# Projections, values, router and gate regrouped by rows of weights; features ahead of values

## The reference

```
h = patches(x) @ W.T + b                                  # 768 -> 192
h = h + attn0(layernorm(h))                               # random-feature attention, 12 heads of 16
h = h + experts(layernorm(h))                             # 4 groups x 8 experts, 2 groups chosen, 2 experts in each, hidden 768
h = h + attn1(layernorm(h))                               # rotated queries/keys, causal softmax, 12 heads of 16
h = h + gated_ffn(layernorm(h))                           # shared + 8 gated experts of width 128, 2 chosen

# attn0: q, k, v = split(x @ w_inp + b_inp); s = (q or k) * 16**-0.25 @ omega.T (16 features)
#        f = exp(s - sum(s)/2 - max(s)) + 1e-6; out = causal linear attention(qf, kf, v) @ w_out + b_out
# attn1: q = rope(x @ Wq + bq); k = rope(x @ Wk + bk); v = x @ Wv + bv
#        out = softmax(causal(q k.T / 4)) v @ Wo + bo
```

## Time and profile before

| what | us |
|---|---|
| median of three runs | 474.67 |
| the three runs | 462.99, 477.31, 474.67 |
| span of the profiled execution | 450.5 |
| TensorE busy in that span | 379.3 (84%) |
| vector engine busy | 142.9 (32%) |
| ScalarE busy | 117.0 (26%) |
| GpSimd busy | 71.0 (16%) |

### The profile page before, as it was taken

One profiled execution on the slowest core, in us unless ns is written; L12 is line 12 of the kernel. 1 busy time (PEld: TensorE's weight loads), 2 busy tenths in 40 slices (PEclk: granted clock), 3 DMA queues, 4 the chain that ended last, 5 costly groups with the idle time before them and its releaser, 6 DMA issues. The chain is left out here.

```text
span 450.5 us, 7352 instructions
## 1 busy us (share of the span) xinstructions
PE 379.3 (84%) x2586; PEld 289.1 (64%) x2586; DVE 142.9 (32%) x408; ACT 117.0 (26%) x311; POOL 71.0 (16%) x115
## 2 busy tenths in 40 slices
PE   0879986975587999999999999999910997889995
PEld 0672555954554888888888888888810476753553
DVE  0450025375722111111111111111107558446544
ACT  1301103324023222333322222333210114531110
POOL 0130001000274021122222222222222200000000
PEclk9995556695555899999999999999985796968999
DMA  7649999300023088888889888888213000000001
GB/s 165 155 89 305 243 314 276 74 1 0 25 94 118 8 269 265 259 257 259 274 264 268 263 278 263 256 261 247 90 46 112 1 1 3 1 0 0 1 0 36
DMA packets 66249, 65.81 MB, mean 146 GB/s; under 512 B 10153, under 2 KB 59889, under 8 KB 66225
## 3 DMA queue, kind: packets, MB, share of 16 engines
q1 hardware_dynamic: 63456, 59.39, 46.9%
q0 software_dynamic: 2400, 5.45, 3.3%
q10 hardware_dynamic: 368, 0.66, 0.7%
HBM read 53.45 MB, written 12.03 MB: 145 GB/s over the span
## 5 line engine op out<-in xcount | busy, mean ns | idle before, releaser
L589 ACT ACTIVATE turned<-ps,b1T 128x128 f32<-128x128 f32 x204 | 56.4, 375 | 125.6 <-PE ps L815 125.6
L831 PE MATMUL ps<-w,turned 128*128 128x192 f32 x408 | 71.9, 326 | 0.0
L811 PE MATMUL ps<-fexp,w 128*128 128x128 f32 x408 | 70.1, 295 | 0.0
L831 PEld LDWEIGHTS ps<-w,turned 128*128 128x128 f32 x408 | 65.5, 190 | 0.1
L811 PEld LDWEIGHTS ps<-fexp,w 128*128 128x128 f32 x408 | 55.8, 193 | 8.4 <-issue 0.2
L815 PE MATMUL ps<-fexp,w_tail 64*128 64x128 f32 x408 | 50.5, 324 | 0.0
L1110 DVE COPY fexp<-ps 128x256 f32<-128x256 f32 x34 | 14.4, 425 | 104.3 <-PE ps L801 101.3
L500 POOL DMA_INDIRECT y_picks<-fexp,y_row x34 | 33.1, 974 | 40.5 <-POOL y_row L496 24.7
L815 PEld LDWEIGHTS ps<-fexp,w_tail 64*128 64x128 f32 x408 | 30.9, 186 | 12.5 <-issue 0.4
L648 PE MATMUL ps<-cst,xn 128*128 128x128 f32 x32 | 8.6, 411 | 28.0 <-DVE xn L910 27.8
L1121 DVE COPY fexp<-ps 128x192 f32<-128x192 f32 x34 | 12.2, 358 | 55.9 <-PE ps L831 55.9
(11 more groups left out here) (216 smaller groups left out, 452.9 us busy)
## 6 DMA issues: line engine op xcount, KB each, us to landing
w<-in_L_ffn_W SPq DMA_DIRECT2D x34, 576.0 KB, 5.4
w<-in_L_ffn_W SPq DMA_DIRECT2D x34, 384.0 KB, 3.2
w_tail<-in_L_ffn_W SPq DMA_DIRECT2D x68, 96.0 KB, 3.7
x_slots<-empty_row SPq DMA_DIRECT2D x1, 6039.5 KB, 25.9
qkT<-x_slots SPq DMA_DIRECT2D x34, 128.5 KB, 4.5
early<-in_x SPq DMA_DIRECT2D x6, 256.0 KB
early<-in_L_ffn_w SPq DMA_DIRECT2D x3, 512.0 KB
qk_padT<-y_picks SPq DMA_DIRECT2D x4, 384.0 KB, 5.0
```

What stands on the lines that cost most here:

```text
L589: last = act.activation(hidden[:, u % 2, c, :], ps[:, 2 + 2 * (u % 2) + c // 3, (c % 3) * P:(c % 3 + 1) * P], ACT.Gelu, bias=b1T[:, c, bas ...
L811: nc.tensor.matmul(ps[:, 2 + 2 * buf + half, c * P:(c + 1) * P], w1[:, u, (c + 3 * half) * P:(c + 3 * half + 1) * P], x_rowsT[:, buf, 0, : ...
L831: last = nc.tensor.matmul(ps[:, 6 + u % 2, 0:D], hidden[:, u % 2, c, :], w2[:, u, c, :], start=(c == 0), stop=(c == KH - 1))
```

## The change

- `load_columns_twice` loads the 64-row parts of both attentions' query, key and value weights a second time into partitions 64 to 127 (one DMA more for the first attention, three for the second); the router's 64-row parts likewise (two more).
- The projections first do all full-row matmuls of a group and then the half-row ones, alternately on the lower and the upper half of the rows. This holds for L723, L658, L741, L845 and L854. Router and gate results get a PSUM bank for each tile or each parity.
- The output projections use 128 rows for both parts; the lower part of `wo` is filled with zeros by two vector memsets at the start.
- In the first attention the transpose of omega comes first and the values after the features; the vector engine's `values_out(0)` moves behind its feature work. The padded transposes use banks 4, 5 and 0, 1 instead of 4, 5 and 6, 7; the first scores wait for all four copies.
- `values` signals once at its end instead of after each half.

```diff
         def load_columns(q, dst, src, done):
             q.dma_start(dst[:, 0, :], src[0:DA, :]).then_inc(done, 16)
             q.dma_start(dst[0:DB, 1, :], src[DA:D, :]).then_inc(done, 16)
+        def load_columns_twice(q, dst, src, done):
+            load_columns(q, dst, src, done)
+            q.dma_start(dst[DB:P, 1, :], src[DA:D, :]).then_inc(done, 16)
...
             def values(wv):
                 w = wv.rearrange("p c (j q d) -> p c q j d", q=2, d=HD)
+                def dst(b, q):
+                    return ps[q * SEQ:(q + 1) * SEQ, 6 + b // 4, (b % 4) * (D // 2):(b % 4 + 1) * (D // 2)]
                 for b in range(NIMG):
                     for q in range(2):
-                        dst = ps[q * SEQ:(q + 1) * SEQ, 6 + b // 4, (b % 4) * (D // 2):(b % 4 + 1) * (D // 2)]
-                        for c, rows in ((0, DA), (1, DB)):
-                            last = nc.tensor.matmul(dst, xnT[0:rows, c, b * SEQ:(b + 1) * SEQ], w[0:rows, c, q],
-                                                    start=(c == 0), stop=(c == 1))
-                    if b % 4 == 3:
-                        last.then_inc(v_mm, 1)
+                        nc.tensor.matmul(dst(b, q), xnT[:, 0, b * SEQ:(b + 1) * SEQ], w[:, 0, q], start=(b % 4 == 0), stop=False, skip_group_check=True)
+                for k in range(NIMG // 2):
+                    for b in (k, k + 4):
+                        rows = slice(b // 4 * DB, (b // 4 + 1) * DB)
+                        for q in range(2):
+                            last = nc.tensor.matmul(dst(b, q), xnT[rows, 1, b * SEQ:(b + 1) * SEQ], w[rows, 1, q], start=False, stop=True, skip_group_check=True)
+                last.then_inc(v_mm, 2)
...
             def attention(a):
                 for t in range(NT):
                     pe.wait_ge(qk_pad_ready, NT * a + t + 1)
-                    if a == 0 and t == 1:
-                        pe.wait_ge(v_sb, 4)
...
                     if t == 0:
-                        pe.wait_ge(qk_padT_sb, NT * a + (3 if a else 1))
+                        pe.wait_ge(qk_padT_sb, NT * a + (3 if a else NT))
...
+                pe.wait_ge(wo_zeroed, 2)
                 for t in range(NT):
                     pe.wait_ge(attT_sb, NT * a + t + 1)
-                    for c, rows in ((0, DA), (1, DB)):
-                        last = nc.tensor.matmul(ps[:, 2 * t, 0:D], attT[0:rows, t, c, :], wo[a][0:rows, c, :], start=(c == 0), stop=(c == 1))
+                    for c in range(2):
+                        last = nc.tensor.matmul(ps[:, 2 * t, 0:D], attT[:, t, c, :], wo[a][:, c, :], start=(c == 0), stop=(c == 1))
                     last.then_inc(proj_mm, 1)
...
+            nc.tensor.transpose(ps[:, 3, 0:HD], omega8[:, :, :].rearrange("f h d -> f (h d)"), ident[0:HD, 0:HD]).then_inc(omega_mm, 1)
             for c in range(3):
-                for k, rows in ((0, DA), (1, DB)):
-                    last = nc.tensor.matmul(ps[:, c, :], wqkv0[0:rows, k, c * P:(c + 1) * P], xnT[0:rows, k, :], start=(k == 0), stop=(k == 1))
-                last.then_inc(qkT0_mm, 1)
-            values(wqkv0[:, :, 2 * D:3 * D])
-
-            nc.tensor.transpose(ps[:, 3, 0:HD], omega8[:, :, :].rearrange("f h d -> f (h d)"), ident[0:HD, 0:HD]).then_inc(omega_mm, 1)
+                nc.tensor.matmul(ps[:, c, :], wqkv0[:, 0, c * P:(c + 1) * P], xnT[:, 0, :], start=True, stop=False)
+            for c in range(3):
+                rows = slice(c % 2 * DB, (c % 2 + 1) * DB)
+                nc.tensor.matmul(ps[:, c, :], wqkv0[rows, 1, c * P:(c + 1) * P], xnT[rows, 1, :], start=False, stop=True).then_inc(qkT0_mm, 1)
             pe.wait_ge(omega_sb, 1)
             pe.wait_ge(qkT0_sb, 3)
...
+            values(wqkv0[:, :, 2 * D:3 * D])
             attention(0)
...
-            for t in range(NT):
-                pe.wait_ge(xnT_sb, 2 * NT + (NT if t == 3 else t + 1))
-                for k, rows in ((0, DA), (1, DB)):
-                    last = nc.tensor.matmul(ps[:, t, 0:2 * D], xnT[0:rows, k, t * P:(t + 1) * P], wqkv1[0:rows, k, 0:2 * D], start=(k == 0), stop=(k == 1))
-                last.then_inc(qk_mm, 1)
+            for pair in range(0, NT, 2):
+                for t in (pair, pair + 1):
+                    pe.wait_ge(xnT_sb, 2 * NT + (NT if t == 3 else t + 1))
+                    nc.tensor.matmul(ps[:, t, 0:2 * D], xnT[:, 0, t * P:(t + 1) * P], wqkv1[:, 0, 0:2 * D], start=True, stop=False)
+                for t in (pair, pair + 1):
+                    rows = slice(t % 2 * DB, (t % 2 + 1) * DB)
+                    nc.tensor.matmul(ps[:, t, 0:2 * D], xnT[rows, 1, t * P:(t + 1) * P], wqkv1[rows, 1, 0:2 * D], start=False, stop=True).then_inc(qk_mm, 1)
...
             up1(1, 1, True)
+            pe.wait_ge(score_ready, 1)
             down1(0, 0, True)
-            pe.wait_ge(score_ready, 1)
...
+            for a in range(2):
+                dve.memset(wo[a][DB:P, 1, :], 0.0).then_inc(wo_zeroed, 1)
...
-            dve.wait_ge(pads_zeroed, 5)
-            values_out(0)
             dve.wait_ge(omega_mm, 1)
...
+            dve.wait_ge(pads_zeroed, 5)
+            values_out(0)
             attention(0)
```

More of the change, by code:

```diff
@@ L244, in vit_tower @@
         wtok_dma, ident_dma, const_dma, attn0_dma, attn1_dma = sem("wtok_dma"), sem("ident_dma"), sem("const_dma"), sem("attn0_dma"), sem("attn1_dma")
-        pads_zeroed = sem("pads_zeroed")
+        pads_zeroed, wo_zeroed = sem("pads_zeroed"), sem("wo_zeroed")
         x_by_col_ready = [sem(f"x_by_col_ready{c}") for c in range(NCH)]
@@ L346, in _ @@
             load_row(sp, btok[:, :], dram["L0_tok_b"], attn0_dma)
-            load_columns(sp, wqkv0, dram["L0_attn_w_inp"][0], attn0_dma)
+            load_columns_twice(sp, wqkv0, dram["L0_attn_w_inp"][0], attn0_dma)
             sp.dma_start(bqk0[:, :], dram["L0_attn_b_inp"][0:2 * D].rearrange("(c p) -> p c", p=P), allow_slow_non_contiguous=True).then_inc(attn0_dma, 16)
@@ L355, in _ @@
             for n, name in enumerate(("L1_attn_Wq", "L1_attn_Wk", "L1_attn_Wv")):
-                load_columns(sp, w1v[:, :, n * D:(n + 1) * D], dram[name], attn1_dma)
+                load_columns_twice(sp, w1v[:, :, n * D:(n + 1) * D], dram[name], attn1_dma)
             load_row(sp, bqk1[:, 0:D], dram["L1_attn_bq"], attn1_dma)
@@ L364, in _ @@
             pw = dram["L0_ffn_Wge"].rearrange("g d e -> d g e")
-            for c, (a, b) in enumerate(((0, DA), (DA, D))):
-                sp.dma_start(wroute[0:b - a, c, 0:G], dram["L0_ffn_Wg"][a:b, :]).then_inc(route_dma, 16)
-                sp.dma_start(wroute[0:b - a, c, G:G + NE].rearrange("p (g e) -> p g e", g=G), pw[a:b]).then_inc(route_dma, 16)
+            for rows, c, (a, b) in ((slice(0, DA), 0, (0, DA)), (slice(0, DB), 1, (DA, D)), (slice(DB, P), 1, (DA, D))):
+                sp.dma_start(wroute[rows, c, 0:G], dram["L0_ffn_Wg"][a:b, :]).then_inc(route_dma, 16)
+                sp.dma_start(wroute[rows, c, G:G + NE].rearrange("p (g e) -> p g e", g=G), pw[a:b]).then_inc(route_dma, 16)
             sp.dma_start(broute[:, 0:G], dram["L0_ffn_bg"].unsqueeze(0).to_broadcast([P, G])).then_inc(route_dma, 16)
@@ L597, in _ @@
             act.wait_ge(gate_mm, 1)
-            act.activation(score[:, :, :].rearrange("p t e -> p (t e)"), ps[:, 4, 0:NT * E1], ACT.Sigmoid).then_inc(score_ready, 1)
+            act.activation(score[:, :, :].rearrange("p (t b) e -> p b t e", b=2), ps[:, 4:8:2, 0:NT // 2 * E1].rearrange("p b (t e) -> p b t e", e=E1),
+                           ACT.Sigmoid).then_inc(score_ready, 1)
             def silus(n, u, first=False):
@@ L739, in _ @@
                 pe.wait_ge(xnT_sb, NT + t + 1)
-                for k, rows in ((0, DA), (1, DB)):
-                    last = nc.tensor.matmul(ps[:, 0, t * (G + NE):(t + 1) * (G + NE)], xnT[0:rows, k, t * P:(t + 1) * P], wroute[0:rows, k, :],
-                                            start=(k == 0), stop=(k == 1))
+                nc.tensor.matmul(ps[:, t, 0:G + NE], xnT[:, 0, t * P:(t + 1) * P], wroute[:, 0, :], start=True, stop=False)
+            for t in range(NT):
+                rows = slice(t % 2 * DB, (t % 2 + 1) * DB)
+                last = nc.tensor.matmul(ps[:, t, 0:G + NE], xnT[rows, 1, t * P:(t + 1) * P], wroute[rows, 1, :], start=False, stop=True)
             last.then_inc(logits_mm, 1)
@@ L850, in _, with gate_out @@
             turn_tokens(3)
+            def gate_out(t):
+                return ps[:, 4 + 2 * (t % 2), t // 2 * E1:(t // 2 + 1) * E1]
             for t in range(NT):
                 pe.wait_ge(xnT_sb, 3 * NT + t + 1)
-                for k, rows in ((0, DA), (1, DB)):
-                    last = nc.tensor.matmul(ps[:, 4, t * E1:(t + 1) * E1], xnT[0:rows, k, t * P:(t + 1) * P], gate_wT[0:rows, k, :], start=(k == 0), stop=(k == 1))
+                nc.tensor.matmul(gate_out(t), xnT[:, 0, t * P:(t + 1) * P], gate_wT[:, 0, :], start=(t < 2), stop=False, skip_group_check=True)
+            for t in range(NT):
+                rows = slice(t % 2 * DB, (t % 2 + 1) * DB)
```

(11 more changed lines are left out.)

## The result

The changed kernel takes 429.09 us (median of four, 427.16 to 434.10), the kernel before 468.83 on the same chip (median of four, 457.04 to 477.31). The ratio is 0.932 with a 95% interval of 0.921 to 0.942, 6.8% faster; like all ratios here, it leaves out executions more than 1.5% above the shortest of their kernel. On the 474.67 of the prediction that is 442.2, 4 us under the forecast and inside its range. The executions of the kernel before spread far more than those of the changed one; the experiments say how much of that is shown.

The account below looks back on a forecast made before the run. TensorE at half clock was taken to bound the first attention, in a chain of serial stages. Terms -17.5 - 0.6 - 1.5 - 7.2 - 0.6 - 1.2 = -28.6 us, from the median 474.67 to 446; range 434 to 457.

Parts of the forecast that it names:

- to the first scores: First attention: grouped matmuls and values after the features start the scores at 61.1 instead of 78.62 us, -17.5.
- output projection, first: First attention's output projection: unbroken matmuls leave the vector chain of each tile as the bound, -0.6 us.
- second attention to first scores read: Second attention: values no longer late, first scores read at 366.2 instead of 373.36 us, -7.2.
- Rival (a): First attention: the clock rises to 2.4 GHz, -34 us in all, time 440; chance 0.22.
- Rival (d): Experts: staying at 1.2 GHz costs up to 5 us a tile; eight tiles make it slower, 485 us; chance 0.03.
- What a change of rows costs: Regrouped matmuls: each change between full-row and half-row weights was put at 0.3 us in the first attention.
- rival (c): Regrouped matmuls: pairs don't overlap and the gap isn't the row change; 469 us, no change; chance 0.05.
- at 1.2 GHz throughout: First attention: clock stays at half speed, features start at 45.4, values end at 55.0, scores start at 61.1 us.
- Router and gate: Router and gate matmuls: 2.9 us each instead of 4.47 and 4.10, saving 1.5 and 1.2.
- the prediction's own signs of being wrong: Wrong if L658 takes 0.3 or more per two instructions, scores lag features by over 8, or untouched stages' clock differs.
- Its span is 12.5 under the fastest and 24.2 under the median: Whole kernel: profiled span 450.5 us against executions of 462.99 (fastest) and 474.67 (median); the forecast starts from the median.
- Rival (b): Stage from 88.2 us and second attention's front: the clock falls where it was full, 5 us each, 456; chance 0.15.

Follow-up runs that it names:

- Experiment 2: Changed kernel with the first attention's old order: 430.33 us, ratio 0.925; kernel before with the new order alone, matmuls ungrouped: 462.24 us beside 465.27.
- experiment 6: Changed kernel with idle matmuls ahead of the experts: nine during routing, 431.61 us; then only two, before the last wait for the scatter, 427.16 us, ratio 0.921.
- Experiment 7: Changed kernel with SyncE holding the experts' first weights and all later loads until the first attention's scores are done: 429.94 us.
- experiment 5: Changed kernel with the second attention's values alone in the old interleaving of row counts: 437.14 us.
- experiment 1: Kernel before, run again without an edit: six executions, 458.94 to 480.72 us, median 476.34.
- Experiment 4: Kernel before with 20 idle matmuls in TensorE's wait before the second attention: 462.40 us beside 471.36, ratio 0.990; the same in the changed kernel: 432.31 us.

## Why the prediction was right, and where it missed

Profile against profile the change brought 24.5 us, where the sum said 28.6. That is one pair of executions; the other profile of the changed kernel is 7.4 longer. Step by step:

| step | forecast | measured | from |
|---|---|---|---|
| embedding | 0 | +0.4 | projections 35.06, 35.45 |
| to the first scores | -17.5 | -21.9 | 78.62, 56.71, with the row above |
| pause in the scores, and after it | 0 | +2.8 | output projection 94.20, 75.06 |
| output projection, first | -0.6 | -0.7 | next turning 100.58, 80.72 |
| router | -1.5 | -2.1 | logits read 107.18, 85.24 |
| routing, scatter | 0 | +0.4 | first expert 144.73, 123.24 |
| experts | 0 | +5.9 | combine 340.10, 324.49 |
| second attention to first scores read | -7.2 | -6.5 | 373.36, 351.22 |
| output projection, second | -0.6 | -0.7 | next turning 398.35, 375.52 |
| gate | -1.2 | -1.4 | sigmoid 404.50, 380.25 |
| tail | 0 | -0.3 | span 450.5, 426.0 |

(the first row is contained in the second)

Two of the misses, -4.4 in the first attention and +5.9 in the experts, are both the clock and nearly cancel. That is luck: the forecast had neither, rivals (a) and (d) had one each. The forecast was for -28.6 from the median; between the medians it came to -40, by the ratio to -32.5 of 474.67, between the profiles to -24.5.

**What a change of rows costs** was read rightly. Experiment 2 shows the grouping to be nearly all of the gain, and the pairs overlap: 0.89 us for 32 instructions that the unpaired kernel does in 1.54. At full clock the values of the second attention took 9.91 us with 31 changes of rows and take 3.1 grouped but unpaired, 0.22 a change; that holds what two column halves side by side save as well. So rival (c) is out, and in experiment 2 the order alone brought the first scores 11.3 us sooner, not its 5 or 6 (with a clock that rose, which (c) did not have).

**First attention.** The step that failed is the one in its heading, "at 1.2 GHz throughout". Rival (a) came true for a part, 38.4 to 52: features started at 42.86, not 45.4, the vector engine followed 0.94 behind, not 1.68, and so began at 43.80, not 47.1, and the values were over at 48.0, not 55.0, so that the first two tiles' transposes were done long before they were needed. These are the extra 4.4 us. No profile holds the changed order's projections at 0.50 throughout; in experiment 6, where the clock rose at 41.5, the first scores came 1.2 later. The vector chain was forecast at 7.8 us and took 7.8 (43.80 to 51.64).

**The pause in the scores** was put at nothing. From the first score instruction to the end of the scores it is 7.9 us, against 5.6 before, and 0.5 more go to the transposes behind, at half clock until 69.1: 2.8 in all. Experiment 7 shows that the pause comes with the weights that SyncE loads meanwhile. The change moved the scores from 78.6 to 56.7 us, into the time of these loads.

**Router and gate.** 2.6 and 2.7 us in all for TensorE, forecast 2.9 each. The second groups took 1.07 and 1.03, so halves overlap. The Trainium skill's rule for weight loads ("TensorE: Matmul & The Clock Gate", LDWEIGHTS) gave an estimate of 1.6; the router's first group alone took 1.58, against an estimate of 0.86 by the rule (8 x 107 ns), so the measurement decides against using it at half clock.

**Second attention.** Right to 0.7 us, by its own mechanism; experiment 5 prices the values at 4.1 at full clock.

**The experts** were taken to be untouched. Rival (d) named the place and was right in kind: they were entered at 0.50 for 14 us rather than 4.4 and paid 5.9, a fifth of what it needed to turn the sign. This is also one of the prediction's own signs of being wrong, a granted clock that differs in a stage that the diff doesn't touch. Experiment 6 shows it: with the clock up the stage is 193.8. It isn't the change's doing in particular, since experiment 1 found 15 us of it in the kernel before.

**"Its span is 12.5 under the fastest and 24.2 under the median"** is the step that hid the rest. I took this for what lies around a span. It is 1.85 us. For the execution of experiment 1 the remainder, 24.7 us, was shown to be clock; for the others only the mean clock is known, 0.844 in the profile, 0.825 to 0.849 in the lower group and 0.781 to 0.806 in the upper. The sum was made on the luckiest execution of the kernel before. Experiment 4 ties the upper group to the second attention: filled with idle matmuls, the median falls by 9 us. The changed kernel has no projection left that changes rows at each matmul, and its four executions lie 7 us apart instead of 20. The gain by medians is 40 us, that between the two profiles 24.5, which itself holds the two clock terms above. That the difference is granted clock is argued from experiments 1 and 4, not shown. What an execution of 464 us looks like stays open: none of that group was profiled without an edit. The one with the fill, 462.2 us, had half clock from 377 to 418, in scores, weighted values and output projection.

**Rival (b)**, the clock falling where it was full, did not cost in the first attention (69.1 to 82.7 at 1.00, as before). The Trainium skill's remark on pauses between bursts (same page, Why this matters for your kernels) agrees in kind: the clock fell at 52, within a wait of 3.2 us. In the second attention it was 0.50 from 352.4 to 362.6, and the stage from the first scores read to the next turning still took 24.3 us, against 25.0 before.

## What to carry to other kernels

Group matmuls by how many rows of weights they use: here a change cost some 0.2 us at full clock and 0.2 to 0.3 at half, more than a small matmul itself, and the broken stream stayed at half clock for 28 us of full occupancy. Put half-row ones on alternate halves where that is free; the pairs overlap, but their worth on the whole kernel was within the spread. Where there is a choice, try an unbroken full-row piece in front of the long one: in experiment 2 the long one got the full clock by it. Compare the profiled span with the times before a sum is made on it: only some 2 us of such a gap were overhead here, and where the rest was looked into, it was another clock.

## What the runs showed of the hardware

- 28 us of back-to-back matmuls with a change of rows at each did not raise the granted clock from 0.50 (first attention before, in all three profiles of it; in experiment 1 also the 28.8 us of the second), while within or behind an unbroken piece of full-row matmuls it rose to 1.00 (the projections' 4.27 us in the changed kernel, the features' 4.44 in experiment 2, the idle matmuls' 3.54 in experiment 6). Two stretches don't fit a simple rule. In the first profile the clock rose at 353.9, 2.6 us into the alternating projections, behind 1.9 us of transposes. And in experiment 1 the weighted values, unbroken and all on 128 rows, ran at 0.50 from 405.6 to 411.7 without a rise. That the rows are what matters, and not the size of the matmuls, was not tried by itself. The Trainium skill ("TensorE: Matmul & The Clock Gate", What's actually happening) says that sustained activity releases it; TensorE's busy time as the profile counts it does not tell which stretch will be released.
- Four score instructions on distinct tiles take 0.12 us at half clock (5.87/192 x 4), and 32 half-row ones of 96 columns in four quadrants 0.89 at full clock.
- With the DMA engines full of data, TensorE stood still for 1.15 to 3.05 us in the middle of a group, in the nine profiles that have the scores in the time of the weight loads (1.81 in the order-only kernel), around a transfer of 16 KB of code; with the data held back a transfer of code still came, and there was no pause. A smaller one, 0.42 us, is in experiment 1 (81.34), where the scores come later.
- Two idle matmuls of 512 columns, 3.5 us of work without a result, returned 7 us in the 34 expert tiles behind them, profile against profile; by the medians 2 to 4 were left of it.
